# Ring places at an image's border, the first load and the tail, and the dilated band's add on TensorE, in a four-stage image kernel

## What is computed

```python
x = x + _L0_conv_ref(_gn(x))      # 3x3 maximum (dilation), border value -2
x = x + _L1_conv_ref(_gn(x), ...) # selective scan (below)
x = x + _L2_conv_ref(_gn(x), L2_conv_weight, L2_conv_bias)  # 3x3 convolution
x = x + _L3_conv_ref(_gn(x), L3_conv_weight, L3_conv_bias)  # 3x3 convolution

def step(h, inputs):              # in L1, over 64*64 tokens; h is (batch, 256, 32)
    dt_t, x_t, B_t, C_t = inputs
    h = h * jnp.exp(dt_t[..., None] * A) + (dt_t * x_t)[..., None] * B_t[:, None, :]
    y = jnp.einsum('bds,bs->bd', h, C_t)
    return (h, y)
```

## Time and profile before

| | |
|---|---|
| median of 3 runs | 14727.23 us (14719.27 to 14730.22) |
| the profiled execution | 14720.38 us, span from first to last instruction 14718.6 us |
| from the span's start to the first scan | 220.7 us |
| first scan to first scan, 15 image periods | 890.6 to 897.7 us |
| behind the last scan | 195.2 us |
| DVE, POOL, PE, ACT busy | 93%, 92%, 85%, 65% |
| DVE's waits for POOL's `hc`, whole span | 299.4 us in 191 waits, longest 8.1 |

### The profile page before, as it was taken

The page is one execution under the profiler, slowest core; times in us unless marked ns, Lnnn a source line. Parts: engine busy times, 40 slices in busy tenths (PEclk is TensorE's granted clock), DMA queues, the critical chain, the costliest instruction groups (busy, mean ns, idle before and its releaser), DMA issues.

```text
span 14718.6 us, 164375 instructions
## 1 busy us (share of the span) xinstructions
PE 12490.3 (85%) x27626; PEld 4914.0 (33%) x27626; DVE 13645.9 (93%) x11707; ACT 9618.0 (65%) x18363; POOL 13562.3 (92%) x6104
## 2 busy tenths in 40 slices
PE   4888888888888888888888888888888888888886
PEld 1333333333333333333333333333333333333332
DVE  4999999999999999999999999999999999999994
ACT  4666666666666666666666666666666666666664
POOL 4999999999999999999999999999999999999994
PEclk9999999999999999999999999999999999999998
DMA  3344443434434344443444434344343444434442
GB/s 89 110 117 122 116 123 108 126 114 114 123 110 130 108 116 123 114 125 108 117 123 115 123 109 124 116 114 123 110 131 108 114 124 115 125 109 117 124 114 76
DMA packets 1258544, 1701.84 MB, mean 116 GB/s; under 512 B 402220, under 2 KB 551156, under 8 KB 1257268
## 3 DMA queue, kind: packets, MB, share of 16 engines
q1 hardware_dynamic: 1257364, 1689.83, 40.0%
HBM read 1525.80 MB, written 124.13 MB: 112 GB/s over the span
## 4 chain that ended last, share of the span: by engine, by line
PE 29%; DVE 23%; issue 22%; POOL 15%; ACT 5%; DMA 3%; SPq 1%; DVEq 1%; POOLq 1%; ACTq 0%
PE y_ps L1110 17%; DVE h L1248 12%; POOL hc L662 12%; DVE u_in L1232 8%; PE proj_ps L1064 3%; POOL u_in L639 2%; PE side_ps L1121 2%; PE b_ps L1162 2%; DMA c_sb<-bc_dram 2%; DVE vmax L1219 1%; ACT a_ps L852 1%; PE y_ps L1107 1%; PE side_ps L1096 1%; DMA z<-x_dram 1%; PE side_ps L1099 1%
## 5 line engine op out<-in xcount | busy, mean ns | idle before, releaser
L662 POOL TENSOR_TENSOR hc<-h,c_sb 128x1024 f32<-128x1024 f32 x4096 | 9597.7, 2363 | 725.4 <-DVE h L1248 543.1
L1248 DVE TENSOR_TENSOR_SCAN h<-a_ps,carry,u_in 128x512 f32<-128x512 f32 x7168 | 8762.0, 1264 | 284.9 <-POOL hc L662 152.9
L1110 PE MATMUL y_ps<-hc,ident 128*128 128x512 f32 x16400 | 8140.0, 622 | 636.2 <-POOL hc L662 573.4
L852 ACT ACTIVATE a_ps<-dt,a_neg 128x512 f32<-128x512 f32 x8192 | 5575.3, 687 | 4417.2 <-DVE h L1248 4392.4
L1110 PEld LDWEIGHTS y_ps<-hc,ident 128*128 128x128 f32 x16400 | 3118.6, 196 | 4393.1 <-issue 3066.3
L1232 DVE TENSOR_TENSOR u_in<-dtx,b_ps 128x1024 f32<-128x1024 f32 x2816 | 3363.2, 1194 | 82.2 <-PE b_ps L1162 78.8
L639 POOL TENSOR_TENSOR u_in<-dtx,b_sb 128x1024 f32<-128x1024 f32 x1282 | 3032.7, 2366 | 0.1
L1162 PE MATMUL b_ps<-b_parts,select 96*128 96x512 bf16 x2816 | 1114.7, 396 | 1185.2 <-DVE u_in L1232 1183.6
L1248 DVE TENSOR_TENSOR_SCAN h<-a_ps,u_in 128x512 f32<-128x512 f32 x1024 | 1199.6, 1207 | 257.3 <-POOL hc L662 146.5
L1162 PEld LDWEIGHTS b_ps<-b_parts,select 96*128 96x128 bf16 x2816 | 280.2, 99 | 2682.1 <-DVE u_in L1232 2143.0
L1064 PE MATMUL proj_ps<-u_ln,w_x 128*128 128x512 f32 x2064 | 971.6, 593 | 4.6 <-ACT u_ln L804 3.7
(11 more groups left out here) (107 smaller groups left out, 7266.4 us busy)
## 6 DMA issues: line engine op xcount, KB each, us to landing
c_sb<-bc_dram SPq DMA_DIRECT2D x4100, 256.0 KB, 3.2
b_sb<-bc_dram SPq DMA_DIRECT2D x1284, 256.0 KB, 3.2
raw<-x SPq DMA_DIRECT2D x68, 512.0 KB
x_dram<-vmax SPq DMA_DIRECT2D x68, 512.0 KB, 4.6
z<-x_dram SPq DMA_DIRECT2D x68, 512.0 KB, 7.8
out<-raw SPq DMA_DIRECT2D x272, 128.0 KB
x_dram<-x SPq DMA_DIRECT2D x129, 256.0 KB, 3.8
x<-x_dram SPq DMA_DIRECT2D x136, 224.0 KB, 8.1
```

The source lines that it names most:

```text
L662: pool.tensor_tensor(hc[:, ring_at(c * S + s, HC_RING)], h[:, ring_at(c * S + s, H_RING)], c_sb[:, s // C_GROUP % C_RING, s % C_GROUP:s % ...
L852: act.activation(a_ps[:, a_slot(c * S + s, half)], dt[:, c % 2, half], ACT.Exp, scale=a_neg[:, at:at + 1]).then_inc(a_made, 1)
L1110: mm = pe.matmul(y_ps[:, half], ident[:, :], hc[:, ring_at((c * S + s) % (NC * S), HC_RING), half], start=False, stop=(s == S - 1), skip_g ...
L1248: dve.tensor_tensor_scan(h[:, r, half], a_ps[:, a_slot(c * S + s, half)], u_in[:, s % U_RING, half], start, ALU.mult, ALU.add).then_inc(h_ ...
```

## The change

- Rings: the last four steps of an image get the places 0, 1, 0, 2 (`RING_END`, `LAST_IN_RING`). Steps 254 and 0 share a place, 253 and 1, and 255 and 2; 252 and 254 share one too.
- In the loop POOL's `add_dilated` is gone. PE adds each half band into the bank `proj_ps` by two matmuls with the identity, one of `norm`, one of `raw`, at states 26, 27 (half 0) and 29, 30 (half 1) of chunks 1 to 4. ACT copies each half to `vmax` at states 26 and 29 (`copy_dilated`). The store moves from state 21 to 31. The second convolution's first copies into `raw` wait for three bands, the block that meets the last band for all four.
- Ahead of the loop: three quarters of image 0 are loaded by ACT's queue before anything else, the last quarter and the halo rows by SP behind the constants, and the zeros after them; POOL clears two rows of `raw` instead of all. The four bands use two `norm` and two `vmax` tiles in turn (the second pair lies in `h`), with semaphores of their own. x1 is read back band by band, half of the channels by SP and half by ACT. DVE prepares the convolution weights behind the bands, no longer ahead of the load. PE waits for them only before the first `center`.
- Behind the loop: the blocks of the last two convolutions take turns in `side_ps` and `proj_ps`; block k waits for the part of the padded image that it reads; the rows of the first six blocks are stored while the last two are computed, and the rest by SP and ACT, eight transfers each.

```diff
@@ -54,6 +54,7 @@
+RING_END, LAST_IN_RING = 4, (0, 1, 0, 2)
...
@@ -86,7 +87,7 @@
-DIL_SLOTS, ADD_DILATED, STORE_ROWS = (6, 9, 11, 13, 15), 18, 21
+DIL_SLOTS, ADD_DILATED, DILATED_OUT, STORE_ROWS = (6, 9, 11, 13, 15), ((26, 27), (29, 30)), (26, 29), 31
...
@@ -111,6 +112,8 @@
+        if 1 <= c <= BANDS:
+            at_state["dilated", c - 1, half] = ADD_DILATED[half]
...
-    return 0 if use[0] in ("center", "var", "x", "z", "xproj", "dt") else 1
+    if use[0] == "conv_last":
+        return 1 - use[2] % 2
+    return 0 if use[0] in ("center", "var", "x", "z", "xproj", "dt", "dilated") else 1
...
+        in_h = h[:, :, :, :].rearrange("p a b t -> p (a b t)")
+        norms = (norm[:, :, :], in_h[:, 0:(R + 2) * (W + 2)].rearrange("p (r w) -> p r w", w=W + 2))
+        vmaxs = (vmax[:, :, :], in_h[:, (R + 2) * (W + 2):(2 * R + 2) * (W + 2)].rearrange("p (r w) -> p r w", w=W + 2))
...
@@ -347,8 +364,8 @@
-            whole = NC * S // ring * ring
-            return n % ring if n < whole else n - whole
+            whole = (NC * S - RING_END) // ring * ring
+            return n % ring if n < whole else LAST_IN_RING[n - whole]
...
+        def load_raw_rows(engine, image, piece):
...
+            rows = BAND // RAW_PIECES
+            engine.dma_start(raw[:, 1 + piece * rows:1 + (piece + 1) * rows, :],
+                             image_rows(image)[:, piece * rows * W:(piece + 1) * rows * W]).then_inc(raw_in, 16)
...
+        def load_raw_halo(engine, image):
...
+            img = image_rows(image)
+            engine.dma_start(raw[1:P, 0:1, :], img[0:P - 1, (BAND - 1) * W:]).then_inc(raw_in, 16)
+            engine.dma_start(raw[0:P - 1, BAND + 1:, :], img[1:P, 0:W]).then_inc(raw_in, 16)
...
+        def load_first_x1(engine, k, channels):
...
+            engine.wait_ge(first_rows_out[k], 16)
+            for ch in channels:
+                engine.dma_start(x1[ch * R * R:(ch + 1) * R * R, :].rearrange("p (g l w) -> p g l w", l=BANDS, w=TW)[:, :, k],
+                                 x1_dram[ch].rearrange("(g l) r q w -> l (r q) g w", l=BANDS)[k]).then_inc(x1_in, 16)
...
+        def store_rows(engine, image, r, first, last):
...
+            rows = raw[r // R * C * R + r % R:(r // R + 1) * C * R:R, 1 + first:1 + last, :]
+            dst = out[bass.ds(image, 1)].rearrange("o c (g r) w -> r (o c) g w", r=BAND)[r]
+            engine.dma_start(dst[:, first:last], rows).then_inc(stored, 16)
...
-                sp.wait_ge(dil, number * DIL + DIL_AT[k])
+                if number is None:
+                    sp.wait_ge(first_sum, k + 1)
+                else:
+                    sp.wait_ge(dil, number * DIL + DIL_AT[k])
...
-                             vmax[:, :, 0:W]).then_inc(x1_rows_out, 16)
+                             (vmaxs[k % 2] if number is None else vmax)[:, :, 0:W]
+                             ).then_inc(first_rows_out[k] if number is None else x1_rows_out, 16)
...
@@ -496,10 +543,12 @@
-                if k < 2:
+                if k >= 2:
+                    sp.wait_ge(banks[bank_of((conv, n, k - 2))][1], used(b, conv, n, k - 2))
+                if conv == "conv_last":
+                    sp.wait_ge(padded_done, (b * 2 + n) * PAD_PARTS + min(PAD_PARTS, (2 * k + 2) * PAD_PARTS // NB + 1))
+                elif k < 2:
...
-                else:
-                    sp.wait_ge(side_filled, used(b, conv, n, k - 2))
...
+            load_raw_rows(sp, 0, RAW_PIECES - 1)
...
-            sp.wait_ge(setup_v, SETUP_V)
+            load_raw_halo(sp, 0)
...
-            for piece in range(RAW_PIECES):
-                load_raw(0, piece)
+            sp.wait_ge(setup_a, 2)
...
-                store_x1_rows(0, k)
-            sp.wait_ge(setup_a, 2)
-            for part in range(2):
-                load_x1(0, part, range(C))
+                store_x1_rows(None, k)
+                if k:
+                    load_first_x1(sp, k - 1, range(C // 2))
+            load_first_x1(sp, BANDS - 1, range(C // 2))
+            sp.sem_inc(x1_rows_out, BANDS * 16)
...
@@ -582,9 +628,12 @@
-            for k in range(BANDS):
-                store_output(B, B - 1, k, "conv_last")
-            sp.wait_ge(stored, (B + 2) * BAND * 16)
+            for n_done, first, last in ((NC - 2, 0, BAND - 2 * CB), (NC, BAND - 2 * CB, BAND)):
+                for k in range(n_done - 2, n_done):
+                    sp.wait_ge(banks[bank_of(("conv_last", 1, k))][2], read(B, "conv_last", 1, k))
+                for r in range(BAND if first == 0 else BAND // 2):
+                    store_rows(sp, B - 1, r, first, last)
+            sp.wait_ge(stored, (B + 1) * BAND * 16 + 2 * BAND * 16)
...
@@ -594,7 +643,8 @@
-            pool.memset(raw[:, :, :], 0.0).then_inc(setup_p, 1)
+            pool.memset(raw[:, 0:1, :], 0.0).then_inc(setup_p, 1)
+            pool.memset(raw[:, BAND + 1:, :], 0.0).then_inc(setup_p, 1)
...
@@ -619,14 +669,11 @@
-            def add_dilated(number, k):
...
-                last = number * DIL + DIL_AT[k]
-                pool.wait_ge(dil, last - 1)
...
@@ -641,7 +688,10 @@
-                add_dilated(0, k)
+                pool.wait_ge(first_max, 4 * k + 4)
+                add_band(norms[k % 2], vmaxs[k % 2], k).then_inc(first_sum, 1)
+            pool.wait_ge(first_sum, BANDS)
+            pool.sem_inc(dil, DIL - 4)
...
@@ -671,11 +721,11 @@
-                        if 1 <= c <= BANDS and s == ADD_DILATED:
-                            add_dilated(b + 1, c - 1)
...
+            for piece in range(RAW_PIECES - 1):
+                load_raw_rows(act, 0, piece)
...
@@ -872,6 +922,33 @@
+            def normalise_first(k):
...
+                if k == 0:
+                    act.wait_ge(dil, 4)
+                act.wait_ge(setup_v, 3 + NH + TAPS)
+                if k >= 2:
+                    act.wait_ge(first_sum, k - 1)
...
...
+            def copy_dilated(number, k, half):
...
+                act.wait_ge(proj_filled, used(number - 1, "dilated", k, half))
+                rows = slice(half * R // 2, (half + 1) * R // 2)
+                out = act.activation(vmax[:, rows, 0:W].rearrange("p r (q w) -> p r q w", q=R),
+                                     proj_ps[:, :].rearrange("p (r w q) -> p r q w", q=R, r=R // 2), ACT.Copy)
+                out.then_inc(proj_emptied, 1)
+                if half == NH - 1:
+                    act.wait_ge(proj_emptied, read(number - 1, "dilated", k, half))
+                    act.sem_inc(dil, 1)
...
+                    act.wait_ge(dil, (b + 1) * DIL + DIL_AT[BANDS - 2])
+                if use == ("conv", 1, (BANDS - 1) * R // CB):
...
...
@@ -920,9 +1000,12 @@
-                normalise_band(0, k)
-            act.wait_ge(x1_in, X1_DMAS * 16)
+                normalise_first(k)
+            for k in range(BANDS):
+                load_first_x1(act, k, range(C // 2, C))
+            act.wait_ge(x1_in, X1_FIRST * 16)
...
+            act.wait_ge(setup_v, SETUP_V)
...
+                        if 1 <= c <= BANDS and s in DILATED_OUT:
+                            copy_dilated(b + 1, c - 1, DILATED_OUT.index(s))
...
@@ -1016,11 +1101,14 @@
+            for k in range(NC - 2, NC):
+                act.wait_ge(banks[bank_of(("conv_last", 1, k))][2], read(B, "conv_last", 1, k))
+            for r in range(BAND // 2, BAND):
+                store_rows(act, B - 1, r, BAND - 2 * CB, BAND)
...
-            pe.wait_ge(setup_v, SETUP_V)
...
@@ -1085,6 +1173,19 @@
+            def add_dilated(number, k, half, part):
...
+                rows = half * R // 2 + 1
+                if part == 0:
+                    pe.wait_ge(dil, number * DIL + DIL_AT[k] - 1)
+                    take_scratch(number - 1, "dilated", k, half)
+                    pe.matmul(proj_ps[:, :].rearrange("p (r w) -> p r w", w=W), ident[:, :],
+                              norm[:, rows:rows + R // 2, 1:W + 1], start=True, stop=False, skip_group_check=True)
+                else:
+                    pe.matmul(proj_ps[:, :].rearrange("p (r w) -> p r w", w=W), ident[:, :],
+                              raw[:, k * R + rows:k * R + rows + R // 2, :],
+                              start=False, stop=True, skip_group_check=True).then_inc(proj_filled, 1)
...
...
-                    pe.wait_ge(padded_done, (b * 2 + n) * PAD_PARTS + PAD_PARTS)
+                    pe.wait_ge(padded_done, (b * 2 + n) * PAD_PARTS + (PAD_PARTS if name == "conv" else k // 2 + 1))
...
+                    pe.matmul(bank[:, :].rearrange("p (g w) -> p g w", w=W), w_main[n][:, part, :],
...
+                if use[0] == "center":
+                    pe.wait_ge(setup_v, SETUP_V)
...
...
-            own(dve.memset(norm[:, :, :], BORDER))
-            own(dve.memset(spare[:, :], 0.0))
...
+                own(dve.memset(norms[n], BORDER))
...
+            def prepare_weights():
...
+                own(dve.memset(spare[:, :], 0.0))
+                dve.wait_ge(setup_a, 1)
+                own(dve.tensor_scalar(a_neg[:, :], a_neg[:, :], -1.0, None, ALU.mult))
```

(54 more changed lines are left out.)

85 lines of the change are left out of this document (41 added, 44 removed).

## The result

The changed kernel takes 14622.1 us (median), the kernel before 14723.7: a ratio of 0.9933, 95% interval 0.9921 to 0.9944. The forecast was 14547, so 102 us came where 177 were expected.

A forecast was written before the change was run, and what follows sets the result against it. DVE was taken as the bound, with POOL's add hidden. The profiled 14720.4 - 92 + 6 - 63 - 31 gave 14540, and the median lying 6.8 us higher made it 14547 us; range 14475 to 14615.

The forecast's parts named there:

- Part 1, the border: New ring places at the 15 borders between images: 6.1 us saved per border, 92 us in all.
- DVE's way back to the loop's beginning: At the border: DVE needs 2.8 us from its last scan, so the next image's first scan starts at 7376.2.
- What is late next in chunk 0 is ACT ... so this wait moves with it and isn't made longer: Chunk 0, after the border: ACT's 2.66 us wait for `z` moves along with `hc` and does not grow.
- Rival A: Border closes only half, DVE's way back or ACT's decays taking the rest: 2.5 us per border, 14601; chance 0.11.
- E: Rival: step 254 waits for 252, so the border's wait only moves; 0 to 1 us per border, 14630; chance 0.04.
- Part 2, the band: Dilated band moved from POOL to PE and ACT in chunks 1 to 4: 0.1 us per band, 6 us cost.
- Hidden as shown, so nothing is gained: Chunks with bands: removing POOL's 4 adds of 4.02 us per image gains nothing, since DVE is the bound.
- Rival B: POOL's relief pays: `hc` waits at chunk beginnings, about 1 us, go behind four chunks; 64 us, 14483; chance 0.06.
- The price of TensorE: Four added matmuls per band at states 26, 27, 29 and 30: 0.1 us per band, 64 bands, 6 us.
- Part 3, ahead of the loop: Before the first scan: earlier loads save 29.2 us, and from the maxima on 33.7 us; 63 us in all.
- 0.5 MB and the halo's 0.25 MB take 4.7 us: Ahead of the loop: image 0's remaining loads behind the constants land 4.7 us after ACT's table, at 31.6.
- Part 4, behind the loop: After the last scan: 14 and 15 us from the two convolutions, 2 us from the last store; 31 us saved.

The follow-up runs named there:

- pe_price: halo_split with POOL adding the band at step 18 again and PE's four band matmuls still issued, their result thrown away; 14542.5 us, ratio 0.9876.
- pool_adds_split: halo_split with the band's addition back on POOL at step 18 and its store at state 21; 14543.9 us, ratio 0.9880.
- halo_split: The changed kernel with each halo load of 127 partitions cut into one of 112 and one of 15; 14531.8 us, ratio 0.9868.

## Why the prediction was right or wrong

**Part 1, the border (92 us told, 14 measured in the whole loop, the bands included).** The mechanism at the border was right: DVE is 2.02 us late at step 254 (2.4 told), and the first scan starts 0.25 us behind POOL's product of 254 (0.2 told). One term was too long without harm: DVE's way back to the loop's beginning, taken over from PE as 2.8 us, is 2.3 us at most, counted as there from the start of the last scan (in the ninth image from 7304.9 to 7307.22). The failed step is "What is late next in chunk 0 is ACT ... so this wait moves with it and isn't made longer". It named one late work and did not ask what POOL itself would wait for: `c_sb` of step 4, behind the raw loads on SP. What the runs showed in its place: a wait of 3.99 us at step 7 that gives back most of the 4.6. The rows were to be had in the trace of before, where the product of step 4 began as that load landed, 20.0 us behind the first scan, and where SP already took 3.61 us to issue a halo load:

```profile
7400.58 4.68 POOL L662 TENSOR_TENSOR hc<-h,c_sb 128x1024 f32<-128x1024 f32 x2 [0.90 <-DMA c_sb<-bc_dram]
...
7384.90 3.61 SPq L433 DMA_DIRECT2D raw<-x  x1
7389.21 5.19 SPq L468 DMA_DIRECT2D c_sb<-bc_dram  x2
```

SP's queue was looked at for `z` alone. Rival A was right that chunk 0 gives the gain back, and wrong in the cause (ACT). E came nearest to the time, 14630, by luck: the wait did move, but to step 7 and the loads, not to step 254. With the loads cut, the reorder gives 6.4 us per border.

**Part 2, the band (6 us of cost told, a gain of 12 to 35 measured).** "Hidden as shown, so nothing is gained" failed. With the add on POOL, chunks 2 and 3 are 0.3 us longer each, and DVE waits longer for `hc`. My reading, which no run tests, is that the 5.4 us that POOL idles in chunk 2 are not one reserve, while its add of 4.02 us stands at one state. Rival B had the sign, but with 64 us of relief too much of it. The price of TensorE, 0.1 us per band, had the right size: 0.1 and 0.3 us in chunks 2 and 3 of pe_price against pool_adds_split, nothing in the medians.

**Part 3, ahead of the loop (63 told, 54.2 measured).** The rows of after, against the earlier trace rows:

```profile
39.88 0.63 ACT L755 ACTIVATE raw<-raw 128x512 f32<-128x512 f32 x1 [7.07 <-DMA raw<-x]
...
56.67 3.89 DVE L1334 TENSOR_REDUCE vmax<-norm 128x516 f32<-128x1548 f32 x2 [30.65 <-ACT norm L937]
...
98.94 0.63 ACT L755 ACTIVATE x<-x 128x512 f32<-128x512 f32 x1 [21.09 <-DMA x<-x_dram]
```

```profile
19.59 0.28 SPq L417 DMA_DIRECT2D raw<-x  x1
19.91 8.86 SPq L418 DMA_DIRECT2D raw<-x  x1
```

From the maxima to the sum of `x` it is 42.3 us (43.5 told), so the chain of the bands was read rightly. The first sum came at 39.9 and not at 31.6: the term "0.5 MB and the halo's 0.25 MB take 4.7 us", priced by bytes, failed by the same two loads, one of which SP took 8.86 us to issue. The 4.3 MB that the prediction took its rate from held the same two loads; while they ran, the trace of before has this (share of the DMA engines and GB/s last):

```profile
45.00:50.00 5.00, 0.00 (x0) 0.00 (x0) 0.00 (x0) 0.00 (x0) 0.00 (x0) 1.00 0.07 24
```

In halo_split ACT finds the rows landed, without a wait, and the first scan is at 159.2 (158 told):

```profile
32.74 0.62 ACT L756 ACTIVATE raw<-raw 128x512 f32<-128x512 f32 x1
```

**Part 4, behind the loop (31 told, 35.1 measured).** Two blocks of the last convolution, against the earlier trace rows:

```profile
14586.42 2.85 PE L1223 MATMUL proj_ps<-padded,w_main 128*128 128x512 f32 x6
...
14591.99 2.84 PE L1223 MATMUL side_ps<-padded,w_main 128*128 128x512 f32 x6
```

A block takes 5.57 us where it took 6.47; 5.45 to 5.6 were told, and the last scan stands 160 us ahead of the end (164 told).

Of the sum, 75 us are missing in the median. halo_split shows where they were: at 14531.8 it lies 15 us under the forecast, with the border (6.4 us) and the part ahead of the loop as told and the band better than told.

## What to carry to other kernels

When a wait is removed at a place, follow every input of the work behind it to the queue that brings it, and ask for each what that queue does in between; a load that landed just in time in the old trace is the next wait. A load is not priced by its bytes: look at the share of the DMA engines while it runs, and if the number of partitions doesn't divide by 16, cut the transfer so that its larger part does. And two waits that end at nearly the same time have to be closed together: each edit alone looks worthless.

## What the runs showed of the hardware

Two loads over 127 partitions with rows of 1 KB took 10.84 us at 24 GB/s, one row per 43 ns, and 1.79 us when cut into 112 and 15. While they ran, the issues behind them on SP were held too (6.06 us for two of `c_sb`, 8.86 us for the second halo load ahead of the loop), and for some 6 us the DMA engines stood at a share of 0.07: 0.25 MB stopped the loads behind it. It did so wherever it stood, at step 0 and at step 6 of an image. And a TensorE that idles for 10.7 us in a chunk (busy 102.2 of 113.0 us in chunk 2 of the changed kernel) is nearly full for what must be ready in time: 3.4 us of added passes per band cost 2.2 us.
